# Two VectorE tails of a layered gated-attention kernel moved to GpSimd

## The reference, cut to what matters

```python
def _w8a8_linear(x, w, b):
    qx, sx = _dyn_quant(x)
    qw, sw = _quant_weight(w)
    y = jnp.einsum('bnc,oc->bno', qx, qw) * (sx * sw[:, 0])
    return y + b
x = x + jnp.tanh(g_xattn[3]) * _L3_xattn_ref(...)
```

```python
gamma_w = jnp.clip(jnp.mean(jnp.abs(w)), 1e-05, None)
w_dq = jnp.clip(jnp.round(w / gamma_w), -1.0, 1.0) * gamma_w
```

## Time and profile before

| | us |
|---|---|
| median of 3 runs | 2429.48 (2425.93 to 2430.18) |
| the profiled execution | 2448.54 |
| its span, first to last instruction | 2446.4 |
| TensorE busy | 2169.1 (89%) |
| VectorE busy | 1510.5 (62%) |
| ScalarE busy | 1123.7 (46%) |
| GpSimd busy | 743.5 (30%) |

### The profile page before, as it was taken

The page is one execution under the profiler, slowest core; times in us unless marked ns, Lnnn a source line. Parts: engine busy times, 40 slices in busy tenths (PEclk is TensorE's granted clock), DMA queues, the critical chain, the costliest instruction groups (busy, mean ns, idle before and its releaser), DMA issues. The chain is left out here.

```text
span 2446.4 us, 38415 instructions
## 1 busy us (share of the span) xinstructions
PE 2169.1 (89%) x10486; PEld 1377.7 (56%) x10486; DVE 1510.5 (62%) x3702; ACT 1123.7 (46%) x3555; POOL 743.5 (30%) x932
## 2 busy tenths in 40 slices
PE   6969999978799789978999999999998598979999
PEld 3446777855455344445555566566655355545685
DVE  6975434435566577765577677776776588843234
ACT  2022234411355355545555555556554288832242
POOL 5705510045333300013344444444443200003104
PEclk9969999989999899999999999999999599979999
DMA  6902245452400000000000000000000000201143
GB/s 217 310 17 84 92 131 162 155 156 81 172 1 0 3 1 0 0 26 1 1 1 1 0 0 0 0 0 0 0 0 1 4 6 5 107 3 46 63 136 97
DMA packets 85587, 127.18 MB, mean 52 GB/s; under 512 B 12418, under 2 KB 74626, under 8 KB 84226
## 3 DMA queue, kind: packets, MB, share of 16 engines
q1 hardware_dynamic: 75490, 98.52, 12.5%
q0 software_dynamic: 9984, 27.28, 3.5%
HBM read 91.41 MB, written 47.84 MB: 57 GB/s over the span
## 5 line engine op out<-in xcount | busy, mean ns | idle before, releaser
L2375 ACT ACTIVATE l2x_prob<-l2x_pS,l2x_nb,l2x_rms_q 128x256 f32<-128x256 f32 x256 | 142.5, 565 | 116.6 <-DVE l2x_nb L2610 114.8
L1035 ACT ACTIVATE moe_act_g<-moe_pG 128x96 f32<-128x96 f32 (+1 forms) x159 | 53.2, 335 | 279.3 <-PE moe_pU L968 119.8
L1186 PE MATMUL l2x_pQ<-big,l2x_xT 128*128 128x512 f32 x312 | 149.6, 602 | 4.8 <-DVE l2x_part L2588 4.3
L2607 DVE TENSOR_REDUCE l2x_negmax<-l2x_pS 128x2 f32<-128x512 f32 x128 | 87.8, 686 | 92.3 <-PE l2x_pS L2195 89.5
L928 POOL DMA_INDIRECT moe_yk<-route_y,moe_slot_i x72 | 69.6, 966 | 236.7 <-DMA route_y<-moe_y 187.5
L3117 DVE TENSOR_TENSOR l3f_hid<-l3f_act_g,l3f_pA 128x256 f32<-128x256 f32 (+1 forms) x103 | 38.1, 370 | 163.2 <-ACT l3f_act_g L3028 106.4
L2205 PE MATMUL l2x_pOT<-l2x_probT,l2x_v 128*128 128x512 f32 x256 | 124.7, 610 | 4.5 <-ACT l2x_probT L2390 4.5
L2195 PE MATMUL l2x_pS<-l2x_kT,l2x_qT 128*128 128x256 f32 x512 | 128.3, 380 | 0.0
L2941 PE MATMUL l3f_pA<-big,l3f_xnT 128*128 128x512 f32 x256 | 125.4, 614 | 0.0
L2214 PE MATMUL l2x_pT<-big,l2x_oT 128*128 128x256 f32 x512 | 121.1, 379 | 0.7 <-ACT l2x_oT L2383 0.7
L3028 ACT ACTIVATE l3f_act_g<-l3f_pA 128x256 f32<-128x256 f32 (+1 forms) x103 | 35.3, 343 | 183.4 <-PE l3f_pA L2941 183.4
(11 more groups left out here) (499 smaller groups left out, 5812.8 us busy)
## 6 DMA issues: line engine op xcount, KB each, us to landing
route_x<-in_c_zero SPq DMA_DIRECT2D x1, 13184.0 KB, 80.4
moe_xg<-route_x SPq DMA_DIRECT2D x103, 128.0 KB, 2.1
route_y<-moe_y SPq DMA_DIRECT2D x103, 128.0 KB, 1.7
big<-in_e_gu SPq DMA_DIRECT2D x1, 6144.0 KB, 19.2
l3f_xg<-route_x SPq DMA_DIRECT2D x39, 128.0 KB, 2.2
route_y<-l3f_y SPq DMA_DIRECT2D x39, 128.0 KB, 1.7
big<-in_f_gu SPq DMA_DIRECT2D x1, 4096.0 KB, 12.3
big<-in_e_down SPq DMA_DIRECT2D x1, 3072.0 KB, 25.2
```

The costliest lines, as they stand in the source:

```text
L1186: last = pe.matmul(out, lhsT=xT[:, k, :], rhs=w[:, k, cols], start=(k == 0), stop=(k == KC - 1))
L2375: ins = act.activation(prob[g % 2][:, h, :], pS[j][:, (h % 2) * 2 * P:(h % 2 + 1) * 2 * P], ACT.Exp, scale=rms_q[g][:, h:h + 1], bias=nb[: ...
L2607: dve.tensor_reduce(negmax[:, c], pS[j][:].rearrange("p (h k) -> p h k", h=2), AX.X, ALU.max, negate=True).then_inc(S["max_steps"], 1)
```

## The change

**The rounding.** `Ternary.vector` becomes `Ternary.pool`, with four GpSimd instructions in place of three of VectorE: times 1/gamma, clipped, plus ROUND, minus ROUND (as a tensor_tensor with a [P, 3] tile of -ROUND). Each waits for the one before. VectorE keeps `means`. On GpSimd the step stands at the same place of the order, so behind the turn's rstd.

**The output tail.** VectorE's `out` keeps its first instruction, which now multiplies by the step and by the gate; the bias is multiplied by the gate once, when the weights are prepared. The rest is a new step `add` on GpSimd with lag 5, one batch behind `out`: times sw, plus bias, plus x. VectorE's next `out` waits for it, as outp is one tile.

```diff
--- before.py
+++ after.py
@@ -621,6 +621,7 @@
         self.G, self.ps = G, ps
         self.lane, self.total = ph.sb("lane", [1, 3, 16]), ph.sb("w_total", [1, 3])
         self.ones, self.ginv = ph.sb("ones", [1, P]), ph.sb("ginv", [P, 3])
+        self.minus_round, self.round_set = ph.sb("minus_round", [P, 3]), ph.sem("round_set")
         self.tmp = [ph.sb(f"ternary_tmp{i}", [P, 3, self.STEP]) for i in range(2)]
         self.sums_ps, self.sum_steps, self.steps = (ph.sem(n) for n in ("sums_ps", "sum_steps", "ternary_steps"))
 
@@ -651,17 +652,26 @@
         ch(dve.tensor_scalar(gam[:], self.ps[:, 0:3], 1.0 / (P * self.COLS), 1e-5, ALU.mult, ALU.max))
         ch(dve.reciprocal(self.ginv[:], gam[:]))
 
-    def vector(self, dve, b, p):
+    def pool(self, pool, b, p):
 
         w, q, tmp = self.G["l2f_all"], self.G["l2f_all"].bitcast(BF16), self.tmp[p]
-        cols = bass.ds(b * self.STEP, self.STEP)
-        dve.tensor_tensor(tmp[:], w.rearrange("p (m c) -> p m c", m=3)[:, :, cols], bc(self.ginv[:], self.STEP),
-                          ALU.mult).then_inc(self.steps, 1)
-        dve.wait_ge(self.steps, 3 * b + 1)
-        dve.tensor_scalar(tmp[:], tmp[:], 1.0, -1.0, ALU.min, ALU.max).then_inc(self.steps, 1)
-        dve.wait_ge(self.steps, 3 * b + 2)
-        dve.tensor_scalar(q.rearrange("p (m c) -> p m c", m=3)[:, :, cols], tmp[:], ROUND, -ROUND, ALU.add,
-                          ALU.add).then_inc(self.steps, 1)
+        spare, cols = self.G["spare"], bass.ds(b * self.STEP, self.STEP)
+        if isinstance(b, int) and b == 0:
+            pool.memset(self.minus_round[:], -ROUND).then_inc(self.round_set, 1)
+            pool.wait_ge(self.round_set, 1)
+            pool.wait_ge(self.sum_steps, 8)
+        if not (isinstance(b, int) and b < 2):
+            hold(pool, self.steps, 4 * (b - 1), spare)
+        pool.tensor_tensor(tmp[:], w.rearrange("p (m c) -> p m c", m=3)[:, :, cols], bc(self.ginv[:], self.STEP),
+                           ALU.mult).then_inc(self.steps, 1)
+        hold(pool, self.steps, 4 * b + 1, spare)
+        pool.tensor_scalar(tmp[:], tmp[:], 1.0, -1.0, ALU.min, ALU.max).then_inc(self.steps, 1)
+        hold(pool, self.steps, 4 * b + 2, spare)
+        pool.tensor_scalar(tmp[:], tmp[:], ROUND, None, ALU.add).then_inc(self.steps, 1)
+        hold(pool, self.steps, 4 * b + 3, spare)
+        pool.tensor_tensor(q.rearrange("p (m c) -> p m c", m=3)[:, :, cols], tmp[:],
+                           self.minus_round[:].unsqueeze(2).to_broadcast([P, 3, self.STEP]), ALU.add
+                           ).then_inc(self.steps, 1)
 
 
 class NormSplit(NormAll):
@@ -1623,7 +1633,7 @@
                 if isinstance(b, int) and b == 1:
                     tq.clear_blocks(pool)
 
-            pipeline(pool, order, {"stats": stats})
+            pipeline(pool, order, {"stats": stats, "ternary": lambda b, p: ternary.pool(pool, b, p)})
 
         @block.tensor
         def _(pe):
@@ -1680,11 +1690,10 @@
                 if isinstance(b, int) and b == 0:
                     ternary.add_lanes(dve)
 
-            def ternary_part(b, p):
+            def means(b, p):
                 if isinstance(b, int) and b == 0:
                     dve.wait_ge(*G["loaded"]["l2f"])
                     ternary.means(dve)
-                ternary.vector(dve, b, p)
 
             def gate(b, p):
                 dve.wait_ge(qkv_ps, 2 * b + 1)
@@ -1730,7 +1739,7 @@
             pipeline(dve, order, {"stats": lambda b, p: nm.vector(dve, b, p),
                                   "normalise": normalise, "qkv": gate, "pick": pick,
                                   "rows": rows, "divide": divide,
-                                  "ternary": ternary_part, **sm.vector_steps(dve)})
+                                  "ternary": means, **sm.vector_steps(dve)})
 
 
 def phase_l3_attention(nc, D, G):
@@ -1773,7 +1782,7 @@
         order = (("S0", 2), ("P3", 3), ("M0", 2), ("stats", 0), ("V2", 3), ("quantA", 4), ("qk", 1),
                  ("S1", 2), ("v", 1), ("P0", 2), ("M1", 2), ("V3", 3), ("oT", 3), ("rows", 1),
                  ("S2", 2), ("aq", 4), ("M2", 2), ("P1", 2), ("V0", 2), ("turn", 1), ("back", 3), ("normalise", 0), ("quantX", 0),
-                 ("spread", 1), ("S3", 2), ("P2", 2), ("V1", 2), ("out", 4), ("xq", 0), ("M3", 2), ("divide", 3))
+                 ("spread", 1), ("S3", 2), ("P2", 2), ("V1", 2), ("out", 4), ("xq", 0), ("M3", 2), ("divide", 3), ("add", 5))
         block = ph.block()
 
         @block.sync
@@ -1806,7 +1815,18 @@
                 if isinstance(b, int) and b == 1:
                     tq.clear_blocks(pool)
 
-            pipeline(pool, order, {"stats": stats}, peel=6)
+            def add(b, p):
+                if isinstance(b, int) and b == 0:
+                    pool.wait_ge(w_read, 5)
+                pool.wait_ge(out_read, b + 1)
+                pool.tensor_tensor(outp[:], outp[:], sw["o"][:], ALU.mult).then_inc(out_steps, 1)
+                pool.wait_ge(out_steps, 2 * b + 1)
+                pool.tensor_tensor(outp[:], outp[:], bias["o"][:], ALU.add).then_inc(out_steps, 1)
+                hold(pool, out_steps, 2 * b + 2, G["spare"])
+                x = G["x_all"][:, b, :]
+                pool.tensor_tensor(x, outp[:], x, ALU.add).then_inc(added, 1)
+
+            pipeline(pool, order, {"stats": stats, "add": add}, peel=6)
 
         @block.tensor
         def _(pe):
@@ -1930,7 +1950,11 @@
                 wT = pOb.rearrange("p (o i r) -> p i o r", o=KC, i=KC)
                 dve.tensor_copy(qwT[n][:].rearrange("p i (o r) -> p i o r", o=KC), wT).then_inc(w_read, 1)
                 dve.tensor_scalar(sw[n][:], pO[:, C:2 * C], {"q": 0.25, "o": 1.0}[n], None, ALU.mult).then_inc(w_read, 1)
-                dve.tensor_scalar(bias[n][:], W[f"L3_b{n}"][:, 0, :], {"q": 0.25, "o": 1.0}[n], None, ALU.mult)
+                if n == "q":
+                    dve.tensor_scalar(bias[n][:], W["L3_bq"][:, 0, :], 0.25, None, ALU.mult)
+                else:
+                    dve.tensor_scalar(bias[n][:], W["L3_bo"][:, 0, :], G["tg"][:, 3:4], None, ALU.mult
+                                      ).then_inc(w_read, 1)
 
             def stats_of(b, p):
                 if isinstance(b, int) and b == 1:
@@ -1971,14 +1995,8 @@
             def out(b, p):
                 dve.wait_ge(out_ps, b + 1)
                 after(dve, added, b)
-                dve.tensor_scalar(outp[:], pTq[:, 0:C], qa.step[p][:, 0:1], None, ALU.mult).then_inc(out_read, 1)
-                dve.wait_ge(out_read, b + 1)
-                dve.tensor_tensor(outp[:], outp[:], sw["o"][:], ALU.mult).then_inc(out_steps, 1)
-                dve.wait_ge(out_steps, 2 * b + 1)
-                dve.tensor_tensor(outp[:], outp[:], bias["o"][:], ALU.add).then_inc(out_steps, 1)
-                dve.wait_ge(out_steps, 2 * b + 2)
-                x = G["x_all"][:, b, :]
-                dve.scalar_tensor_tensor(x, outp[:], G["tg"][:, 3:4], x, ALU.mult, ALU.add).then_inc(added, 1)
+                dve.tensor_scalar(outp[:], pTq[:, 0:C], qa.step[p][:, 0:1], G["tg"][:, 3:4], ALU.mult, ALU.mult
+                                  ).then_inc(out_read, 1)
 
             pipeline(dve, order, {**sm.vector_steps(dve), "stats": stats_of,
                                   "normalise": lambda b, p: nm.normalise(dve, b, p), "quantX": quant_x,
```

## The result

The changed kernel takes 2422.37 us (median of 9 runs, 2419.64 to 2424.99), the kernel before 2429.48. The ratio is 0.9973, with a 95% interval of 0.9964 to 0.9982: faster by 0.27%, or 7 us. One of the nine runs of the kernel before took 3184.51 us and is left out of the ratio, which is taken to the median of the other eight, 2428.9. The profiled execution after took 2422.84 us, with a span of 2420.7.

The account below looks back on a forecast made before the run. TensorE was busy some 90% of the time, with VectorE's tiny instructions on the turn's path. Terms of -7.4 us (tail) and +6 (rounding) made -1.4: 2428 us against the median of 2429.5, range 2415 to 2438.

Parts of the forecast that it names:

- Part 2, the rounding: phase_l1_ffn: 0.51 us a turn won, 1.04 lost to held VectorE instructions; +0.5 a turn, +6 us over 12 turns.
- What the move gives back: phase_l1_ffn: of VectorE's 1.56 us a turn, the turn gets back TensorE's wait for the exT copy, 0.51 us.
- the held time: phase_l1_ffn's `pick`: GpSimd's chain holds L1700 for 0.42 us and L1703 for 0.62, together 1.04 a turn.
- the interpolation from full operands to one with a repeated operand: GpSimd's 128x384 tensor_tensor in the rounding: 1.0 us, taken between 0.73 for 256 columns and 1.27 for 512.
- the one rate for all tensor_scalar: GpSimd's two rounding tensor_scalar: 1.04 us each, from one row of 2.78 us for 1024 columns; 0.5 to 1.4 kept open.
- whatever its size: VectorE's SBUF-to-SBUF tensor_scalar of any size is held until about 0.2 us before GpSimd's instruction ends.
- Part 1, the tail: phase_l3_attention: VectorE loses 1.43 us a turn; mean 0.55 comes back, -7.2 over 13 turns, -7.4 with the drain.
- 0.20 for att: phase_l3_attention: the keys' projection waits 0.20 us for att, counted as won back in both alternating turns.
- rival (d): phase_l3_attention: GpSimd's three tensor_tensor hold VectorE by 0.5 us a turn; -2 in place of -7.4, 2434 us; chance 0.08.
- (a): phase_l1_ffn: GpSimd's tensor_scalar takes 0.5 us, only L1700 is held; stage +1 to +2 us, 2424 in all; chance 0.18.
- (b): phase_l1_ffn: nothing is held in `pick`; -7.1 us in the stage, -14.5 in all, 2415 us; chance 0.14.
- (c): phase_l1_ffn: GpSimd's two tensor_scalar take 1.4 and 1.3 us; net +1.25 a turn, +15 us, 2437 in all; chance 0.20.

Follow-up runs that it names:

- e3: Changed kernel with GpSimd's four rounding instructions a batch later in their list and ahead of the turn's rstd instructions; ratio 0.9928 to the kernel before.
- e9: Changed kernel with GpSimd's third rounding instruction multiplying by 1 and adding ROUND, in place of adding alone; ratio 0.9935 to the kernel before.
- e8: Changed kernel with fifteen more GpSimd instructions on tiles of their own in one turn of phase_l1_ffn, to time each form; one run, 2424.13 us.
- e7: Changed kernel with ROUND subtracted by a second one-operation tensor_scalar and the last tensor_tensor adding zeros, five instructions for four; one run, 2419.27 us.
- e6: Changed kernel with GpSimd's rounding waiting for the end of `rows` of the same turn; ratio 0.9950 to the kernel before.
- e1: Changed kernel with the output tail of phase_l3_attention put back on VectorE, only the rounding moved; ratio 0.9993 to the kernel before.
- e2: Changed kernel with the rounding put back on VectorE, only the output tail of phase_l3_attention moved; ratio 0.9982 to the kernel before.
- e5: Changed kernel with the edits of e3 and e4 together; 2410.75 us against 2429.14 for the kernel before, ratio 0.9922.
- e4: Changed kernel with GpSimd's three output-tail instructions right behind VectorE's `out` of the same turn, lag 4 for 5; ratio 0.9962 to the kernel before.

## Why the prediction was right or wrong

**The total** was 2428 with a range of 2415 to 2438; measured 2422.4, inside. But the forecast said no measurable change, and it is a small gain of 0.27%. The two terms of the sum were wrong by 8.4 and 3.2 us, in opposite directions, so that the total came as near as it did is in part luck.

**Part 2, the rounding: +6 us forecast, -2.4 measured, of which -0.7 in the turns.** The mechanism was right: VectorE's tiny instructions are held by GpSimd's tensor_tensor, and TensorE waits for it through k_rows. Two terms were mis-sized. What the move gives back was put at 0.51 us a turn; e3 and e9 show 14.27 - 13.55 = 0.72 once nothing is held. The whole of it lies between TensorE's L169 and its projection of v, a stretch of 3.02 and 3.09 us in turn before, and of 2.24 and 2.43 in e3; the wait of the earlier trace rows was only a part of what that stretch had to give. And the held time was put at 1.04, on two instructions; it is 0.64, on one. That came from GpSimd's prices: 1.0, 1.04, 1.04 and 1.0 forecast, 0.82, 0.51, 1.18 and 0.82 measured. The chain was 4.0 us long instead of 4.9, and only its last instruction met `pick`. The net was thus 0.09 us a turn won, not 0.5 lost. The two steps that failed are the interpolation from full operands to one with a repeated operand (for full operands its 1.0 was right, e8), and the one rate for all tensor_scalar. The sentence that 0.3 us decides which instruction they meet held good: in e9 0.67 us were worth nine.

The forecast also held the small instructions under the 1.04 us tensor_scalar to its end; e7 shows that one of 1.17 us makes the first of them 0.46 in place of 1.1, and leaves the tiny tensor_tensor behind it at 0.17. Of the rows it drew on, xn ended at 1401.93, 0.15 us behind the tensor_tensor and not before its end, and "whatever its size" had for small ones only a memset behind it; for GpSimd's tensor_tensor, e6 and e7 bore it out at 256 and 16 columns.

**The fill** (the turns up to the first att). Of the stage's 2.4 us only 0.7 lie in the 15 turns. 1.7 lie ahead of the first att, where the granted clock of TensorE rises from 0.50 to 1.00. That stretch took 41.9 us before, 40.2 in the changed kernel and in e1, but 38.2 in e2, whose phase_l1_ffn is that of before; and it took 39.4 in e3 and, on another chip, 36.6 in e5, which have one and the same phase_l1_ffn. So this stretch moves by 3 us or more where nothing in it is edited, and whether the change has a part in the 1.7 us stays open.

**Part 1, the tail: -7.4 forecast, -4.2 measured.** The forecast turns of 12.5 us are what e4 gives, with 178.2 us for 15 turns, 9 less than before, though the sum took 0.20 for att in both turns where the earlier trace rows shows that wait in one. In the changed kernel the tail holds qa_q and L1984 in every second turn: rival (d), to which I gave 0.08, is true of half the turns. What spoke against it, that most of VectorE's instructions there read PSUM, overlooked that the two it meets don't. "At no cost that I can see" for the second scalar was 0.06 us (0.54 against 0.48); the turns of e4 show none of it. The step that failed is that nothing would be held: the turns gave back 4.5 us in place of 7.2. The drain was missed by the same: batch 14's step gave back 1.0 in place of 1.43, batch 15's end cost 1.5 in place of 1.2. In each of the two, qa_q was held to 0.70 by the tail's last tensor_tensor, 0.4 us.

**The rivals.** (a), a short tensor_scalar, gave 2424 and came nearest to the total; of its two tensor_scalar one was short and one was not. (b), nothing held, is what e3 and e9 make of the rounding: with the tail as it is, 0.9928 and 0.9935 are 2412 and 2413.7 of 2429.5, below the 2415 it was given. (c) needed 2.6 us for the two tensor_scalar, which took 1.69.

## What to carry to other kernels

Work that is moved to an idle engine has to be placed as well as moved: ask which instructions of the other engine run at that time, and whether they are of the forms that were held here, tensor_scalar and tensor_tensor from SBUF to SBUF. Put a GpSimd chain where VectorE reads PSUM, reduces or waits; here the place was worth 12 us and the move 7. Price each form of instruction by itself, since a chain that is 0.7 us shorter may miss the one instruction that costs a whole stage its gain.
